# The order of four queues in the second attention's query and key projections

## The reference, cut to what matters

```python
qkv = einsum('bsd,ed->bse', layernorm(x), w_qkv)      # 1024 x 1536
qkv = clip(qkv, -8.0, 8.0)
q, k, v = split(qkv, 3, axis=-1)
q = _layer_norm(q, q_ln_w, q_ln_b)                    # over all 512 features
k = _layer_norm(k, k_ln_w, k_ln_b)
...                                                   # 32 heads of 16, scores, ALiBi bias, causal softmax, values, w_out
```

## Time and profile before

| | |
|---|---|
| median of three runs | 1924.27 us (1921.77 to 1926.8) |
| the profiled execution's own time | 1923.28 us |
| its span in the profile | 1921.6 us |
| TensorE busy | 1839.7 us, 96% |
| DVE, ACT, POOL busy | 1137.6 us (59%), 475.6 us (25%), 985.5 us (51%) |
| mean granted TensorE clock | 0.979 of full speed |

### The profile page before, as it was taken

One profiled execution on the slowest core, in us unless ns is written; L12 is line 12 of the kernel. 1 busy time (PEld: TensorE's weight loads), 2 busy tenths in 40 slices (PEclk: granted clock), 3 DMA queues, 4 the chain that ended last, 5 costly groups with the idle time before them and its releaser, 6 DMA issues. The chain is left out here.

```text
span 1921.6 us, 27309 instructions
## 1 busy us (share of the span) xinstructions
PE 1839.7 (96%) x10157; PEld 1443.1 (75%) x10157; DVE 1137.6 (59%) x1939; ACT 475.6 (25%) x623; POOL 985.5 (51%) x1148
## 2 busy tenths in 40 slices
PE   6999999999999999999999889998899999998999
PEld 4888888888888888888888768887654444466887
DVE  6674774774865847747747643313676888636601
ACT  4121111221211211212211120002404666643200
POOL 5676755755856747567536345545721221235432
PEclk9999999999999999999999989999986999999999
DMA  2111111111111111111101112201042333011112
GB/s 95 47 55 53 46 46 46 38 49 38 44 49 41 55 30 45 45 46 38 49 17 45 62 59 83 76 23 57 17 75 48 54 58 57 11 34 48 47 49 72
DMA packets 50499, 93.55 MB, mean 49 GB/s; under 512 B 8752, under 2 KB 13488, under 8 KB 50032
## 3 DMA queue, kind: packets, MB, share of 16 engines
q1 hardware_dynamic: 49776, 91.13, 17.2%
q10 hardware_dynamic: 640, 1.31, 0.5%
HBM read 76.15 MB, written 2.10 MB: 41 GB/s over the span
## 5 line engine op out<-in xcount | busy, mean ns | idle before, releaser
L386 POOL TENSOR_TENSOR a_w_l<-a_raw,a_w_h 128x1024 fp32r<-128x1024 f32 x96 | 205.6, 2142 | 8.0
L732 DVE TENSOR_TENSOR x<-x,a_ps 128x1024 f32<-128x1024 f32 x64 | 78.0, 1219 | 167.8 <-PE a_ps L184 167.7
L1624 ACT ACTIVATE a_pr<-a_ps 128x1024 f32<-128x1024 f32 (+1 forms) x192 | 153.3, 812 | 87.5 <-PE a_ps L1831 70.6
L1574 POOL TENSOR_SCALAR_AFFINE_SELECT a_pr<-a_pr 128x256 f32<-128x256 f32 x128 | 52.0, 406 | 214.5 <-ACT a_pr L1624 212.9
L1851 PE MATMUL a_ps<-a_K,a_Q 64*128 64x512 f32 (+2 forms) x384 | 136.5, 449 | 11.5 <-DVE a_mx L1730 8.6
L184 PE MATMUL a_ps<-a_tt_h,a_w_l 128*128 128x512 f32 x376 | 147.0, 391 | 0.0
L183 PE MATMUL a_ps<-a_tt_l,a_w_h 128*128 128x512 f32 x376 | 146.5, 390 | 0.0
L182 PE MATMUL a_ps<-a_tt_h,a_w_h 128*128 128x512 f32 x376 | 146.4, 389 | 0.0
L72 POOL TENSOR_TENSOR tick<-neg_half 128x1 f32<-128x1 f32 x120 | 35.0, 291 | 214.9 <-PE a_ps L184 207.9
L1726 DVE CUSTOM_DVE_ANT_0 a_masked<-a_ps,a_mask 128x384 bf16<-128x384 f32 (+3 forms) x256 | 115.0, 486 | 32.5 <-PE a_ps L1851 31.2
L1851 PEld LDWEIGHTS a_ps<-a_K,a_Q 64*128 64x128 f32 x384 | 66.6, 199 | 85.0 <-DVE a_mx L1730 33.2
(11 more groups left out here) (247 smaller groups left out, 4724.0 us busy)
## 6 DMA issues: line engine op xcount, KB each, us to landing
a_raw<-in_a_wpair SPq DMA_DIRECT2D x96, 256.0 KB, 2.6
f_raw<-in_f_w SPq DMA_DIRECT2D x33, 320.0 KB, 2.9
a_raw_s<-in_a_wout SPq DMA_DIRECT2D x32, 256.0 KB, 2.8
f_raw<-in_f_w SPq DMA_DIRECT2D x32, 256.0 KB, 2.6
a_raw_s<-in_a_wv SPq DMA_DIRECT2D x28, 256.0 KB, 2.6
a_cst<-in_a_cst SPq DMA_DIRECT2D x32, 129.0 KB, 2.3
a_Q<-a_q_h SPq DMA_DIRECT2D x64, 64.0 KB
a_K<-a_k_h SPq DMA_DIRECT2D x54, 64.0 KB
```

What stands on the lines that cost most here:

```text
L386: nc.gpsimd.tensor_tensor(to_l, src, to_h, ALU.subtract).then_inc(done, 1)
L732: nc.vector.tensor_tensor(a, a, units[i], ALU.add).then_inc(s("out_added"), 1)
L1574: nc.gpsimd.affine_select(tri, tri, [[0, 2], [1, P]], ALU.is_ge, 0.0, base=0, channel_multiplier=-1).then_inc(s("selected"), 1)
L1624: nc.scalar.activation(pr[n % SLOTS][:, 2 * i:2 * i + 2, 0:width], S[at % 2][:, :, skip:skip + width], ACT.Exp, scale=0.25).then_inc(s("sc ...
```

## The change

On POOL the lows of a tile's turns come ahead of that tile's moments, and the first, third and fourth of the weight splits follow tiles 8, 11 and 12 in place of 9, 12 and 13 (the second moves from tile 11 to tile 9). On ACT the highs of the turns of tile m + 2 come ahead of the normalising of tile m. On DVE the wholes of a tile's turns come ahead of its clip and moments. No instruction is added or taken away, and no wait.

```diff
             for m in range(QK):
-                moments(m)
                 for u in units(m):
                     low(u)
-                if m in (9, 11, 12, 13):
-                    if m == 9:
+                moments(m)
+                if m in (8, 9, 11, 12):
+                    if m == 8:
                         pool.wait_ge(qs("proj_done"), NT)
-                    split(2, ((9, 11, 12, 13).index(m),))
+                    split(2, ((8, 9, 11, 12).index(m),))
...
             for m in range(3 * NT):
-                for u in units(m):
+                for u in units(m + 2):
                     high(u)
                 if m < QK:
                     r = m % R
...
             for m in range(AFTER):
                 r = m % R
+                for u in units(m):
+                    whole(u)
                 if m < QK:
                     dve.wait_ge(qs("proj_done"), m + 1)
...
                 else:
                     take_v(m)
-                for u in units(m):
-                    whole(u)
                 if m == QK - 1:
```

## The result

| | before | after |
|---|---|---|
| median | 1924.63 us (20 runs) | 1920.67 us (20 runs, 1916.02 to 1924.86) |
| ratio | | 0.9974, 95% interval 0.9965 to 0.9983 |
| profiled span | 1921.6 us | 1916.8 us |
| mean granted clock | 0.979 | 0.978 |

Faster, by 5.0 us (3.3 to 6.7) as the ratio has it, and 4.0 by the medians. One of the 20 runs of before, at 2077.93 us, was a slow one, and the ratio leaves it out; the other 19 span 1920.77 to 1930.85. The forecast was 6.9 us less, 1917.4; the median stands 3.3 us above it, inside the range. The 0.26% lie just under the 0.3% that the prediction called measurable, so by its own limit the second of its three cases came (no change that can be told), though the interval holds 0.3% and lies clear of no change.

The account below looks back on a forecast made before the run. TensorE, busy in 96% of the span, bounds the kernel. Of 9.57 us lost to waits and clock, new waits of 1.8 and 0.9 leave 6.9 won: profiled 1916.4, median 1917.4 us, range 1913 to 1921.8.

Parts of the forecast that it names:

- the second of its three cases: Measured time within 0.3% of before, no change that can be told: chance 0.39.
- The cause of the waits: Projections: a turn's parts are late because work for later tiles is queued ahead of them; three waits, 7.4 us together.
- The three waits: TensorE waiting for DVE's `full` at turns 2, 6 and 10: 2.30, 1.55 and 3.52 us idle, all to go.
- two new ones: TensorE waiting for ACT's `cl`, behind POOL's full list: 1.8 us at turn 8, 0.9 us at turn 12.
- 8 x 1.26 + 5 x 1.16 + 2 x 1.98 = 19.8 us: POOL's list from low 0 to tile 11's moments: 8 lows, 5 moments, 2 weight splits, never idle, done at 1377.9.
- The clock's 1.65 us: Projections, after turn 10's wait: time lost to TensorE's lower clock, expected to be won back with that wait.
- So the fourth edit is paid back here: Earlier weight splits on POOL end at 1383.0, before tile 16 wants them at 1384.5; left in place, they would end too late.
- The part by part argument: Replay of the queues by half: waits of 2.5, 1.7 and 3.7 us won; clips behind wholes free, TensorE waiting six tiles back.
- I cost the rest at nothing: Behind the projections: the next stretch starts 6.9 us sooner and nothing of that is lost afterwards.
- Rival 3: POOL, now the late engine, 5% to 10% slower than its rows; gain only 3.5 to 5 us; chance 0.15.
- rival 2: Clock falls at turn 8, gain 5.3 us, or later in the stage, 2 to 3; chance 0.22.
- rival 4: Turn 8's wait keeps the clock down through tiles 14 to 21; 25 us of it gives 5 us slower; chance 0.06.

Follow-up runs that it names:

- the last tile first: The whole change, but at tiles 11 and 15 DVE clips ahead of wholes and POOL takes moments ahead of lows; 1917.05 us, ratio 0.9956.
- less work for POOL: The whole change, with ACT in place of POOL making the high parts of the v weights; 1917.2 us, ratio 0.9952.
- each step placed by hand: The whole change's instructions, with the lists of POOL, ACT and DVE written out step by step where the replay finds no wait; 1915.65 us, ratio 0.9948.

## Why the prediction was right, and where its numbers were off

- **The cause of the waits: right.** Highs queued behind later tiles' normalising. The ACT edit alone takes the stretch from 45.1 to 38.9 us.
- **The three waits go, two new ones come at turns 8 and 12: right,** in place and in kind. The sizes were a little low. From starts, turn 8 came 24.84 us behind turn 0 (forecast 24.6) and turn 12 14.00 behind turn 8 (forecast 13.6). The term that was mis-sized is POOL's list: "8 x 1.26 + 5 x 1.16 + 2 x 1.98 = 19.8 us" measured 20.3 (1360.10 to 1380.40), and from there to the moments of tile 15 it took another 14.0, where 13.6 were forecast. The terms leave out that each `moments` starts some 0.09 us after whatever stands ahead of it on POOL (1362.73 - 1360.10 - 2.54 = 0.09 at the first of them); five of them make 0.45 of the 0.5. Of the forecast's 6.9 us in the stretch 6.28 came.
- **The clock's 1.65 us: right in size,** and counting it in full held in all three profiles. That it lies behind turn 10 is luck in part: in one of the three it came behind turn 2 instead.
- **"So the fourth edit is paid back here": wrong.** Tile 16 waits 1.4 us without it and turn 8 1.8 us less; with POOL's list full, the end is the same (38.89 against 38.84 us). The step took the two waits as separate costs. Both hang on one list of POOL that has no idle time, and then a wait further ahead only takes its length off the later one.
- **The part by part argument gave DVE's edit a share it doesn't have,** and called the clips behind the wholes free. They are free for TensorE's banks, not for the tiles' own way around the engines. Alone the edit costs 10 us in the stretch; with ACT's it undoes the gain; with POOL's beside them both it does no harm.
- **"I cost the rest at nothing": neither confirmed nor refuted.** The stretch gives 6.2 us, the ratio 5.0 (3.3 to 6.7). These two agree within the interval, so it isn't shown that anything is given back. The pieces of the maxima took 0.9 us more on the mean of three profiles, with more time at the lower clock; with three of either kernel this stays open. The other kernels show no rule: by ratio and in the stretch the last tile first gives 8.5 and 8.7 us, less work for POOL 9.2 and 8.8, each step placed by hand 10.0 and 9.5, but ACT's edit alone 4.2 and 6.2. Nor do single spans tell: before the stretch turn 0 stands at 1354.19 in one profile and 1356.47 in the other, 2.3 us of the 6.3 that its spans don't show.
- **Rival 3, a slower POOL,** came at 2.5%, 0.5 us on 20, below its 5 to 10%. **Rivals 2 and 4** didn't show in the projections, where the clock stayed up. The later half of rival 2, a fall further on in the stage, did come in two of the changed kernel's three profiles, in the maxima; but two of the three of the kernel before have one there too. The measured 4.0 to 5.0 us lie inside the gains of rivals 2 and 3 as well, so the time alone would not tell them from the forecast. The waits and the stretch do.
- **Two small sums are off.** In rival 4, 6.9 / 0.47 is 14.7 us and not 14.5, and 5 us slower than the median of 1924.27 is 1929; the 1928 counts from the profiled execution. Neither touches the forecast.

## What to carry to other kernels

When a chain crosses engines twice, find the engine whose list holds the second round's part behind later tiles' first round, and move only that one; here one line on ACT gave the whole gain of the stretch, 6.2 us. Moving the same part ahead on an engine that has to wait for it puts the first round behind that wait, and can cost more than the change wins. When one engine's list has no idle time left, order it by who is waited for first: the last member of a group ahead of work that has slack.

## What the runs showed of the hardware

The lower level of TensorE's clock did not go by the length of a single wait: it came behind waits of 2.27, 2.33 and 2.54 us, stayed away behind others of 3.51, 2.30 and 1.80, and came behind 3.5 in two of three profiles of the kernel before. The Trainium skill (TensorE: Matmul & The Clock Gate, What's actually happening) puts the lower level behind an idle window, and says that this window is free-running and isn't set by the kernel's start. That waits of 3.5 us had either outcome agrees with the second statement. The falls behind 2.27 to 2.54 us came behind shorter waits than the first asks for, and there the measurement decides.

A pair of low parts' subtractions on POOL took 2.52 to 2.55 us in the kernel before and 2.53 to 2.55 in the changed one. The pair at 1389.25 in the kernel before had DVE busy beside it for 0.4 us and took 2.52. Those at 1360.10, 1363.88 and 1376.59 in the changed kernel had DVE busy beside them throughout and took 2.54, 2.55 and 2.53. So DVE's wholes and clips cost POOL at most 0.03 us a pair. The prediction had bounded this cost by 0.5 us in all and taken it as nothing, and that holds.
